# Merging routing with the expert stage, and running four shared-expert groups before the experts

## The reference

```
x = x + layernorm(attention(layernorm(x)))          # random-feature attention, 16 heads
X = layernorm(x)                                     # 8192 x 512
idx, w = top 4 of 32 experts per token by sigmoid(X @ gate_w.T) + bias; w normalised
xe[e, slot] = X[token]                               # at most 512 slots an expert
ye = (silu(xe @ W1[e]) * (xe @ W3[e])) @ W2[e]       # hidden width 256
out[token] = sum over its 4 choices of w * ye[expert, slot]
out = out + (silu(X @ sw1.T) * (X @ sw3.T)) @ sw2.T  # the shared expert, every token
x = x + layernorm(out)
```

## Time and profile before

| What | Value |
| --- | --- |
| Median of three runs | 2157.99 us |
| Profiled execution, its own time | 2154.41 us |
| Its span in the trace | 2152.6 us |
| PE, DVE, ACT, POOL busy | 85%, 56%, 52%, 36% |
| Granted TensorE clock, mean | 0.944 of full speed |

### The profile page before, as it was taken

One profiled execution on the slowest core, in us unless ns is written; L12 is line 12 of the kernel. 1 busy time (PEld: TensorE's weight loads), 2 busy tenths in 40 slices (PEclk: granted clock), 3 DMA queues, 4 the chain that ended last, 5 costly groups with the idle time before them and its releaser, 6 DMA issues. The chain is left out here.

```text
span 2152.6 us, 33711 instructions
## 1 busy us (share of the span) xinstructions
PE 1828.6 (85%) x12976; PEld 890.7 (41%) x12976; DVE 1205.9 (56%) x2230; ACT 1124.9 (52%) x1371; POOL 772.0 (36%) x718
## 2 busy tenths in 40 slices
PE   8899999999979999799888898404999988987995
PEld 6444444444427877133333333202444444433342
DVE  7676667666650000158878888831444434435887
ACT  5564555545425665577777776402444444432443
POOL 0000000000000000025677788874777777751110
PEclk9999999999989999899999999756999999998998
DMA  7435353546238886578777875322789999876994
GB/s 257 144 123 187 108 200 106 163 148 211 90 113 220 212 211 160 131 182 238 217 213 221 249 219 169 137 72 90 168 194 267 250 257 227 176 138 169 352 343 155
DMA packets 187791, 403.05 MB, mean 187 GB/s; under 512 B 33780, under 2 KB 72052, under 8 KB 171008
## 3 DMA queue, kind: packets, MB, share of 16 engines
q1 hardware_dynamic: 83184, 222.41, 35.2%
q10 hardware_dynamic: 67584, 122.17, 16.3%
q0 software_dynamic: 36864, 56.32, 13.7%
HBM read 237.06 MB, written 174.98 MB: 191 GB/s over the span
## 5 line engine op out<-in xcount | busy, mean ns | idle before, releaser
L258 PE MATMUL s_proj<-s_xT,keep_wqkv 128*128 128x512 f16 x1536 | 341.8, 379 | 0.0
L1271 POOL DMA_INDIRECT slot_dram<-s_filled,s_slots x256 | 305.2, 1192 | 95.1 <-issue 72.9
L1415 POOL DMA_INDIRECT acc_dram<-s_y,s_slot x128 | 205.9, 1609 | 101.3 <-DMA acc_dram<-s_y,s_slot 47.1
L906 PE MATMUL s_y<-keep_wo,s_at_hl 128*128 128x512 f16 x768 | 194.7, 408 | 42.6 <-ACT s_z L997 42.6
L258 PEld LDWEIGHTS s_proj<-s_xT,keep_wqkv 128*128 128x128 f16 x1536 | 147.8, 98 | 183.2 <-issue 12.6
L237 PE MATMUL s_proj<-keep_wqkv,s_xT 128*128 128x512 f16 x768 | 179.7, 393 | 34.5 <-ACT s_xT L500 34.5
L1522 ACT ACTIVATE s_gate<-s_gates 128x512 f32<-128x512 f32 x96 | 57.3, 597 | 281.2 <-PE s_ups L1474 219.1
L339 POOL TENSOR_SCALAR s_rstd<-s_mv 128x4 f32<-128x4 f32 x16 | 16.0, 998 | 496.5 <-DVE s_mv L354 496.5
L518 ACT ACTIVATE s_hl<-s_rot 128x1024 f16<-128x1024 f32 x64 | 67.6, 1057 | 221.1 <-DVE s_rot L400 220.6
L1577 DVE SCALAR_TENSOR_TENSOR s_h<-s_gate,s_ups 128x512 f32<-128x512 f32 x96 | 65.9, 686 | 199.0 <-ACT s_gate L1522 199.0
L676 ACT ACTIVATE s_phi<-s_logits 128x1024 f32<-128x1024 f32 x128 | 131.1, 1024 | 84.5 <-PE s_logits L697 84.5
(11 more groups left out here) (164 smaller groups left out, 3217.0 us busy)
## 6 DMA issues: line engine op xcount, KB each, us to landing
s_x<-x_in SPq DMA_DIRECT2D x32, 1024.0 KB, 9.8
qk_dram<-s_hl ACTq DMA_DIRECT2D x32, 1024.0 KB
keep_ahead<-qk_dram SPq DMA_DIRECT2D x48, 512.0 KB
acc_dram<-s_zero SPq DMA_DIRECT2D x17, 1024.0 KB, 11.5
v_dram<-s_v ACTq DMA_DIRECT2D x16, 1056.0 KB, 5.8
s_v<-v_dram SPq DMA_DIRECT2D x16, 1056.0 KB
s_spread<-share_dram SPq DMA_DIRECT2D x64, 256.0 KB, 4.6
x_dram<-s_x ACTq DMA_DIRECT2D x16, 1024.0 KB, 4.9
```

The lines of the kernel that those rows point to most:

```text
L258: mm = nc.tensor.matmul(out[:, 512 * b:512 * b + 512], left, right, start=(c == 0 and i == 0), stop=(c == EC - 1 and i == 2))
L906: mm = nc.tensor.matmul(y[m % 2][:], at_hl[n % 2][:, s, c, a * P:(a + 1) * P], keep["wo"][:, w, c, :], start=(c == 0 and i == 0), stop=(c ...
L1271: nc.gpsimd.indirect_dma_start(out=io["slot"], out_offset=bass.IndirectOffsetOnAxis(ap=slots[n % 2][:, a * K + j:a * K + j + 1], axis=0), ...
L1415: nc.gpsimd.indirect_dma_start(out=io["acc"], out_offset=bass.IndirectOffsetOnAxis(ap=slot[e % RING][:, a, 0:1], axis=0), in_=y[e % 2][:, ...
```

## The change

Both stages become one block, with no barrier and no clearing of semaphores between them. Each engine runs its routing program and then its expert program; the new tiles lie on the memory of the routing stage's tiles, except `slots` and `filled`, which POOL still reads and which now have a place of their own. On PE, ACT, DVE and SP the expert program begins with `wait_routed`. POOL goes on with its scatters, and SP alone waits for their landing (`wait_slots`), after it has issued the shared weights, the transposes of groups 0 to 7 and the weights of experts 0 and 1.

The 48 passes get a new order: first the shared expert of groups 0 to 3 (NS = 4), then the 32 experts, then the shared expert of groups 4 to 15. An early group's result goes from `y` to its rows of `acc` by a plain store on ACT's queue (`store_early`). In combine the four early groups need no pass: their `acc` is measured as it is loaded. They stand among the others in `ORDER`. SP's prefetches move: `x1` at e = 3, 8, 13, 18, 23, the transposes of groups 8 to 11 at e = 5, 10, 15, 20.

```diff
+        def wait_routed(eng):
+            eng.wait_ge(position_ready, NG)
+            eng.wait_ge(slots_ready, NG)
+            for k in range(2):
+                eng.wait_ge(xT_stored[k], 16 * NG // 2)
+                eng.wait_ge(rows_stored[k], 16 * NG // 2)
+            for r in range(XS):
+                eng.wait_ge(x_stored[r], 16 * ((NG - 1 - r) // XS + 1))
+        def wait_slots(eng):
             for k in range(2):
-                pool.wait_ge(scattered[k], 16 * A * K * NG // 2)
+                eng.wait_ge(scattered[k], 16 * A * K * NG // 2)
...
+        NS = 4
+        ORDER = (4, 5, 0, 6, 7, 1, 8, 9, 2, 10, 11, 3, 12, 13, 14, 15)
... SP
+            wait_routed(sp)
+            load_shared(0)
+            for w, name in ((sw1, "sw1"), (sw3, "sw3"), (sw2, "sw2")):
+                sp.dma_start(w[:], ...).then_inc(sw_loaded, 16)
+            for n in range(1, NS):
+                load_shared(n)
+            for e in range(2):
+                load_weights(e)
+            for n in range(NS, XTS):
+                load_shared(n)
+            wait_slots(sp)
             for e in range(AHEAD):
                 load_slot(e)
             for e in range(NE):
...
-                if 8 <= e < 8 + XTS:
-                    load_shared(e - 8)
-                if 18 <= e < 18 + X1S:
-                    load_x1(e - 18)
+                if e % 5 == 3 and e // 5 < X1S:
+                    load_x1(e // 5)
+                if e % 5 == 0 and 5 <= e < 25:
+                    load_shared(XTS + e // 5 - 1)
... POOL, add(e)
+                if e == 0:
+                    for k in range(2):
+                        pool.wait_ge(y_stored[k], 16 * NS // 2)
... PE
+            wait_routed(pe)
+            up(0)
+            for p in range(NS):
+                if p + 1 < NS:
+                    up(p + 1)
+                for a in range(A):
+                    down(p, a)
             for a in range(A):
                 turn(0, a)
-            up(0)
+            up(NS)
... ACT
+            def store_early(p):
+                act.wait_ge(y_copied, A * (p + 1))
+                act.dma_start(io["acc"][p * G:(p + 1) * G, :]..., y[p % 2][:]).then_inc(y_stored[p % 2], 16)
... DVE
+            def copy_early(p):
+                if p >= 2:
+                    dve.wait_ge(y_stored[p % 2], 16 * (p // 2))
+                for a in range(A):
+                    dve.wait_ge(y_ready, A * p + a + 1)
+                    nc.vector.tensor_scalar(y[p % 2][:, a, :], ys[a % 2][:], 1.0 / H_SCALE, None, ...)
...
+            for q, n in enumerate(ORDER):
+                p = NE + n
+                if q >= 1:
+                    make_shift(q - 1)
+                if n >= NS:
+                    ...                      # hidden, include, low, measure, add as before
+                else:
+                    for a in range(A):
+                        measure(q, a)
+                    add(q - 1)
+                aggregate(q)
```

More of the change, by code:

```diff
@@ L755, in skewed, with attend_and_route_programs @@
         tile(T // P // 8 - 1, j)
-def attend_and_route_stage(nc, io, keep):
-    with ExitStack() as ctx:
-        t = Tools(nc, ctx, "s4")
+def attend_and_route_programs(nc, io, keep, t):
+    with ExitStack() as tiles:
+        t.ctx = tiles
         PHIS, XS = 4, 3
@@ L1549, in _ @@
                 for i in range(IC):
-                    silu(e + 1, i)
-                    make_high(e + 1, i)
+                    silu(NS + e + 1, i)
+                    make_high(NS + e + 1, i)
                 if e + 2 < NE:
                     turn(e + 2)
-            for n in range(NG):
-                if n + 1 < NG:
+            for q, n in enumerate(ORDER):
+                p = NE + n
+                more = n >= NS and p + 1 < PASSES
+                if more:
                     for i in range(IC):
[L1557 to L1564, removed]
+                        silu(p + 1, i)
+                    make_high(p + 1, 0)
+                if q >= 1:
+                    scale(q - 1)
+                if more:
+                    make_high(p + 1, 1)
+                if q >= 1:
+                    store(q - 1)
             scale(NG - 1)
@@ L1630, in _ @@
                 low(0, i)
+            for p in range(NS):
+                if p + 1 < NS:
+                    for i in range(IC):
+                        hidden(p + 1, i)
+                        low(p + 1, i)
+                copy_early(p)
+            for i in range(IC):
+                hidden(NS, i)
+                low(NS, i)
             for e in range(NE):
                 for i in range(IC):
-                    hidden(e + 1, i)
-                    low(e + 1, i)
+                    hidden(NS + e + 1, i)
+                    low(NS + e + 1, i)
@@ L1658, in _, with attend_route_and_expert_stage @@
             make_shift(NG - 1)
             add(NG - 1)
+    return sp_program, pe_program, act_program, dve_program, pool_program
+def attend_route_and_expert_stage(nc, io, keep, before):
+    with ExitStack() as ctx:
+        routing, experts = Tools(nc, ctx, "s4"), Tools(nc, ctx, "s6")
+        sp4, pe4, act4, dve4, pool4, wait_routed, wait_slots = attend_and_route_programs(nc, io, keep, routing)
+        for stack in before:
+            stack.close()
+        sp6, pe6, act6, dve6, pool6 = expert_and_combine_programs(nc, io, keep, experts, wait_routed, wait_slots)
+        block = ctx.enter_context(nc.Block())
+        @block.sync
+        def _(sp):
+            sp4(sp)
+            sp6(sp)
+        @block.tensor
+        def _(pe):
+            pe4(pe)
+            pe6(pe)
+        @block.scalar
+        def _(act):
+            act4(act)
+            act6(act)
+        @block.vector
+        def _(dve):
+            dve4(dve)
+            dve6(dve)
+        @block.gpsimd
+        def _(pool):
+            pool4(pool)
+            pool6(pool)
@@ L1685, in build @@
         keep["ahead_loaded"] = Tools(nc, ctx, "keep").sem("ahead_loaded")
+        for name, shape, dt in (("slots", [P, A * K], U32), ("filled", [P, A, K, 2], F32)):
+            keep[name] = [ctx.enter_context(nc.sbuf_tensor(f"keep_{name}{k}", shape, dt)) for k in range(2)]
         with ExitStack() as attention:
```

257 lines of the change are left out of this document (134 added, 123 removed).

## The result

The changed kernel takes 2170.8 us, the median of 14 runs (2161.96 to 2193.59), against 2158.97 for the kernel before beside it (14 runs): ratio 1.0066, interval 1.0035 to 1.0097. It became 11.8 us slower where 11.0 us less were forecast, and 2170.8 lies above the range. The profiled execution took 2180.38 us, with a span of 2178.6.

The account below looks back on a forecast made before the run. The prediction saw three limits: the hand-over with PE idle, experts paced by POOL and its DMA, combine by DVE with PE close. Terms −9.0 + 0 − 3 + 1 = −11.0 took 2154.4 to 2143.4 us, range 2126 to 2163.

Parts of the forecast that it names:

- Combine loses four passes: In combine, the steps of the four early groups shrink from 11.45 to 7.3 us each: −16.6 us.
- PE's clock takes 7.6 back: In combine, PE idles in early groups' steps, its clock drops and `include` waits 1.9 us, four times: +7.6 us.
- Early passes end at 1479.5, and the experts start no sooner: In the hand-over, four early passes fit before the experts, whose start stays where it was: 0, between −3 and +6 us.
- Loads and stores on other queues: ACT's early stores and SP's group and weight loads in the hand-over delay nothing: 0 us.
- Experts: Among the experts, 13 prefetches of 1 MB become 9 and three weight loads go: −3, between −8 and +4.5 us.
- Combine's transfers: In combine, a DMA shortfall of some 4 us is covered by five buffers loaded ahead: 0, +4 without that cover.
- the end: After the last store, a second clearing of semaphores and barrier: +1 us, between 0 and +3.
- the first one: Rival: in combine PE's clock holds and among the experts the adds recover, giving 2130.8 us; chance 0.26.
- The adds did not stay at 15.10: Second rival: among the experts, adds fall behind early and stay 15.10 us apart, giving 2165.6 us; chance 0.13.
- The third: Rival: in the hand-over, DVE's `low` instructions and memsets block POOL's scatters, experts start 5.5 us later, 2148.9 us; chance 0.11.

Follow-up runs that it names:

- e1: The changed kernel again, nothing edited: 2162.74 us against 2156.73 for the kernel before, ratio 1.0035.
- e8: The changed kernel with only the first of each token's four scatters sent, output not the reference's; no total time given, early passes 49.6 us.
- e4: The changed kernel without early passes (NS = 0), all sixteen shared passes in combine: 2145.03 us, ratio 0.9952 to the kernel before.
- e5: The kernel before, unchanged, profiled again: 2176.45 us in its one run.
- e11: The changed kernel without early passes (NS = 0), a second time: 2142.91 us, ratio 0.9927 to the kernel before.
- e10: The kernel before with only its prefetches spread, one 1 MB load per two experts: 2158.15 us, ratio 0.9984.
- e9: The changed kernel with one early pass instead of four: 2137.67 us, ratio 0.9889 to the kernel before.
- the execution of the rows: The kernel before, unchanged, in the profiled execution on which the prediction rests: 2154.41 us.

## Why the prediction was wrong, point by point

1. *Combine loses four passes* (−16.6). Right in mechanism and size: an early group's step takes 7.21 us after (7.3 forecast).
2. *PE's clock takes 7.6 back.* The clock falls as forecast; the price was too high. After, DVE's shifts around an early group (2022.53 to 2029.74 is its step) and the `include` that waits:

```profile
2022.53 0.16 DVE L1665 SCALAR_TENSOR_TENSOR s_shift<-s_mv,s_rstd 128x4 f32<-128x4 f32 x1 [1.47 <-POOL s_rstd L1440]
...
2029.74 0.16 DVE L1665 SCALAR_TENSOR_TENSOR s_shift<-s_mv,s_rstd 128x4 f32<-128x4 f32 x1 [1.47 <-POOL s_rstd L1440]
...
2041.19 0.16 DVE L1665 SCALAR_TENSOR_TENSOR s_shift<-s_mv,s_rstd 128x4 f32<-128x4 f32 x1 [1.47 <-POOL s_rstd L1440]
...
2042.46 0.69 DVE L1644 SCALAR_TENSOR_TENSOR s_rows<-s_ys,s_rows 128x512 f32<-128x512 f32 x1 [0.47 <-PE s_ys L1502]
...
2053.21 0.16 DVE L1665 SCALAR_TENSOR_TENSOR s_shift<-s_mv,s_rstd 128x4 f32<-128x4 f32 x1 [1.47 <-POOL s_rstd L1440]
```

   The window behind the early group's step, columns as in the earlier trace rows:

```profile
2029.70:2034.50 4.80, 3.31 (x9) 1.04 (x10) 4.76 (x9) 3.93 (x6) 0.00 (x1) 0.54 1.07 364
```

   The granted clock is 0.54 (1.2 GHz most of the time), and DVE waits 0.47 us in the next step but one, 12.02 us instead of 11.45. So 0.57 us of the gain was lost again where 1.9 was forecast (0.7 to 1.3 in e1). Combine took 157.8 to 160.6 us in five executions with four early passes and all scatters, and 172.9 to 174.2 in five with none: −14.7 by the means, against −9.0.
3. *Early passes end at 1479.5, and the experts start no sooner* (0, at most +6). **This is the step that failed.** PE started 9.0 us after the last slots (8 forecast), and undisturbed passes take 49.6 us (e8; 49.5 forecast). What failed is what these were laid against. The forecast took from the earlier trace rows that the transposes would be ready 55.3 us after the last slots, an interval that belonged to one execution: e4, e5 and e11 show 38.4 to 38.8 (e10 51.7), because the last group is routed late and the last scatter starts only 20 to 23 us behind it, 38.3 in the earlier trace rows. Four passes miss that by 9.0 + 49.6 − 38.6 = 20 us. And the passes don't run undisturbed beside the scatters: 84.7 and 66.2 us. The measured term is +38.3 in the one trace, where the last slots came 13.1 us behind the ones ahead and the stalls in the passes are most of it (84.7 − 49.5 = 35.2); in e1 the transposes come 73.9 us behind the last slots, +18.4 against the earlier trace rows and +35.3 against the 38.6 of the other executions, of which 16.6 are stalls. The second expert's `up` came at 1549.92, where 1497 ± 4 was forecast. The routing stage ahead of it was taken as unchanged without a reason given; it moved by +14.6 here, and by +36.1 between the two executions of before.
4. *Loads and stores on other queues* (nothing). Right in the profiled run: SP's loads were out at 1447.8, the slot loads followed the last scatter's start by 2.2 us.
5. *Experts* (−3). Right in sign, too small: 430.4 to 419.8 us between first and last first add, −10.6 (e1 424.8, so −5.6). A prefetch was priced at 0.56 us for a group's transposes, from eight in a row against the two experts right behind them (13.44); against experts between spread loads (12.86) e10 gives 1.9.
6. *Combine's transfers* (nothing), *the end* (+1): 0.90 DMA share without a visible wait, and +0.5.

The rivals: the clock did not hold, but the adds recovered (13.5 us apart on average), so most of the first one's gain came true. The adds did not stay at 15.10. The third named the right pair, scatters beside the passes, with the victim and the mechanism wrong: by the rule of the Trainium skill ("SBUF — State Buffer", section "SBUF: two separate sides") a DVE instruction with two SBUF inputs and a GpSimd instruction that reads SBUF block each other. A `low` has two, yet the one that met the scatters (1459.05 us) didn't slow them, and neither did the memsets, which the rival counted in and which have no input: each scatter took 0.97 us plus 0.30, as alone. What was held up was PE, and in e8, with a quarter of the scatters, not even that.

In all, +14.6 + 38.3 − 11.0 − 16.4 + 0.5 gives the 26.0 us between the two spans. The medians differ by 11.8, since these are single executions: before took 2176.45 us in e5, the changed kernel 2170.26 in the profiled execution of e1. That four early passes cost time and one gains it rests on medians (e1, e4, e9, e11), not on the two traces.

## What to carry to other kernels

A window read from one execution is a sample: before work is laid into it, ask what its two ends depend on, and look at a second execution. Here both hung on the same late increments, and the end also on a queue of scatters, so the window shrank from 55.5 to 38.6 us in three other executions. Fill such a window only as far as its worst case holds, here one pass of four. And price a prefetch by neighbours with and without one, not by a run of prefetches and what comes right behind it.

## What the runs showed of the hardware

With 256 scatters of slots, PE's semaphore increments reached the others up to 29 us after the matmuls' recorded ends, some of them after the last scatter had landed; in the execution of the rows the last group's came 0.01 us behind. Matmuls that follow don't push them out: in e1 PE ran on for 3.5 us behind the first one, and two came together, at 1462.76 and 1462.92. The Trainium skill ("Perfetto Trace Analysis", section "Per-engine timelines") says that a matmul's end in the profile is estimated and that its semaphore update leaves only when PSUM has acknowledged the writes. The rows agree in so far as records end long before the release; which of the two was late here, the matmul or its increment, they can't tell.

The same executions lack semaphore records. Of some 960 increments by ACT and DVE between 1000 and 1380 us, 157 to 201 have none within 0.5 us in the eleven executions with late increments and all scatters, 27 and 32 of some 1045 in the two with a quarter of the scatters, and 3 of 963 in the run of before that the prediction rests on. Among the experts (1540 to 1880 us) all thirteen lack 98 to 131 of some 400, those with a quarter of the scatters too, and the run of the rows none of 397. So the one undisturbed execution with all scatters is also the one whose recording is all but complete. The Trainium skill ("NOTIFIC — the notification-queue block", section "7.1 Overflow: three behaviours, one of which stalls the engine") says that the block that delivers such records, when a queue of it is full, loses records or holds up the engine that makes them. No run here shows whether that happened, whether the recording holds up PE, or whether both suffer from the scatters' many small counts; the kernel that sends the same slots with fewer counts wasn't tried. That stays open.
